# An attention and FFN kernel: the probabilities turned by way of DRAM and VectorE instead of TensorE

## The chip, the core and the metric

The kernel runs on one core of a Trainium2 chip. The time is that of one execution on the device, in microseconds (us). Lower is better. Beside the runs that are timed there is one profiled execution, from which the trace comes; its span runs from the first to the last instruction.

The core has five engines that work from queues of their own: TensorE (PE, matmuls), VectorE (DVE), ScalarE (ACT), GpSimd (POOL) and SyncE (SP), which issues all DMAs here. They wait for each other by semaphores; an instruction that waits holds up all that stand behind it on its engine.

## What is computed

One layer of a transformer on x of shape 8 x 1024 x 512, in float32: attention over segments of 128 tokens with a running memory, a residual and a layer norm, then an FFN with weights of -1, 0 and 1, a residual and a layer norm.

```python
def step(carry, inp):                      # for each of 8 segments, 8 batches, 8 heads
    mem, z = carry
    q_s, k_s, v_s = inp
    sq = jax.nn.elu(q_s) + 1.0
    att_mem = sq @ mem / (sq @ z)
    sk = jax.nn.elu(k_s) + 1.0
    mem = mem + jnp.einsum('bhlk,bhlv->bhkv', sk, v_s)
    z = z + sk.sum(axis=-2, keepdims=True).transpose(0, 1, 3, 2)
    att_dot = jax.nn.softmax(jnp.einsum('bhik,bhjk->bhij', q_s, k_s) * scale, axis=-1)
    att = att_dot @ v_s
    att = gate * att_mem + (1.0 - gate) * att
    return ((mem, z), att)
...
x = _layernorm(x + out @ Wo, axis=-1)
h = jax.nn.relu(jnp.einsum('bsd,fd->bsf', x, quantize(W1)) + b1)     # 512 -> 2048
x = _layernorm(x + jnp.einsum('bsf,df->bsd', h, quantize(W2)) + b2)
```

## The kernel before

**Tiles.** A group is one segment of two batches (`TG` = 2 tiles t of 128 tokens, 256 tokens), and there are `NG` = 32 groups. To keep the accuracy of float32, the operands of the large products are split into two float16 halves, hi and lo: one engine writes hi, another subtracts it and writes lo. The products then need two or three matmuls each.

**Stages of a group g.** `project_qk` (q and k turned, 4 banks of 24 matmuls), `project_v`, `scores`, the row maxima (`score_max`) and the exponentials into `prob`. prob stands with the queries on the partitions; the product with v in `attend` needs it with the keys on the partitions, so it is turned, split into `pt_hi` and `pt_lo`, and multiplied. `read_memory` and `update_memory` work on the running memory. The two results are gated and added (`gate_mix` on POOL) in `att_mem`; this is turned as well, split into `at`, and goes through `project_out`. After the norm (rows, y) come `ffn_up` (eight steps j, each with `h_relu` on ACT and a split by `h_split` on DVE and `h_rest` on POOL) and `ffn_down` (four pieces for each of two tiles).

**Two ways of turning.** sk, att and y are turned without TensorE: 16 DMAs on SP place the 32x32 blocks (`move_blocks`, `move_sk`), and DVE turns each block in place with one STREAM_TRANSPOSE. prob is turned on TensorE, in `turn_p` (L301 to L312): for each tile t and each half (4 heads) four transposes of 128x128 into a PSUM bank. From this bank ACT evicts `pt_hi` (L1091) and DVE writes `pt_lo` (L690).

**Order.** Each engine has one list of calls inside `for g in range(NG + 2)`; the order is written out call by call and differs from engine to engine. Calls with g - 1 and g - 2 work on earlier groups, so several groups are under way at once. In iteration g TensorE does the projections, scores, reads and `attend` of g, `project_out` of g - 1, `ffn_up` 4 to 7 and all of `ffn_down` of g - 2, and last `ffn_up` 0 to 3 of g - 1. The iteration ends with `update_memory(g)`.

**Banks.** `ffn_up` alternates between PSUM banks 0 and 1, `ffn_down` uses 6 and 7. All else takes banks 2 to 5 in turn (`take`), and waits until the previous user of the bank has been read out.

**Head.** The quantised FFN weights are made in iteration 0: 32 blocks are compared with a threshold on DVE and POOL (`compare`), turned on TensorE (`turn_w`) and evicted by ACT (`put_w`).

SP's list in an iteration is: blocks of the next x (`load_blocks`), amax to DRAM, the move of y of g - 1, amax back, the move of sk, the move of att, the two output tiles of g - 2, the load of the rows of g + 2.

## Time and profile before

| | us |
|---|---|
| median of 3 runs | 1944.64 (1944.27 to 1944.66) |
| profiled execution | 1943.67 |
| its span | 1941.8 |

The mean of TensorE's granted clock in the profiled execution was 0.982 of full speed. The trace is read as follows: a row of a timeline gives the start, the duration (of one or of several merged instructions), the engine, the line of the kernel, the operation, what it writes and reads, and how many there are. In brackets stands how long the engine had been idle and what ended that. Matmuls are pipelined: the duration of one is longer than the distance at which they follow each other. DMAs have their issue on SyncE as SPq rows; the time to landing is in a view of its own.

### The profile page before, as it was taken

Reading aid. Unit: us, or ns where it says so; the run is one execution under the profiler, and the core shown is the slowest. Engines: PE = TensorE matmul, PEld = TensorE weight load, DVE = VectorE, ACT = ScalarE, POOL = GpSimd, SP = SyncE. Lnnn points to the kernel's source line nnn. Section 1 sums busy time; section 2 is a strip of 40 time slices with the busy share of each in tenths; the row PEclk is TensorE's granted clock in tenths of the full one; section 3 lists DMA queues with packets and bytes.
Section 4 is the critical chain, followed back from the end, with each engine's and each line's share of the span. In section 5 each row is a group of like instructions: output and inputs, shape, how many; then the busy total and the mean of one; then the engine's idle time right before and its main releaser. Section 6 shows DMA issues by size and latency. Waiting matters only on the chain.

```text
span 1941.8 us, 45054 instructions
## 1 busy us (share of the span) xinstructions
PE 1868.1 (96%) x16671; PEld 1318.0 (68%) x16671; DVE 1460.8 (75%) x2991; ACT 1002.2 (52%) x2426; POOL 822.2 (42%) x806
## 2 busy tenths in 40 slices
PE   5679999999999999999999999999999999999987
PEld 3557776667777666777766677776667776667754
DVE  7877777777777777777777877777787777877753
ACT  5655455555545555555555555545554554555531
POOL 1724434434444443444454344435434444443442
PEclk9689999999999999999999999999999999999999
DMA  8422332332333233333222323323332332332221
GB/s 276 100 37 48 63 62 41 61 60 58 62 65 63 40 59 59 59 61 66 49 52 59 62 58 62 67 46 53 60 61 57 62 67 37 60 63 59 39 41 31
DMA packets 582536, 120.67 MB, mean 62 GB/s; under 512 B 555936, under 2 KB 559920, under 8 KB 581808
## 3 DMA queue, kind: packets, MB, share of 16 engines
q1 hardware_dynamic: 582320, 117.79, 30.2%
q8 instruction: 135, 2.21, 0.6%
q14 instruction: 81, 0.66, 0.2%
HBM read 50.54 MB, written 16.80 MB: 35 GB/s over the span
## 4 chain that ended last, share of the span: by engine, by line
PE 83%; SPq 6%; DVE 5%; DMA 2%; ACT 2%; issue 1%; POOL 1%; POOLq 0%; DVEq 0%; ACTq 0%
PE bank L393 11%; PE bank L394 11%; PE bank L407 9%; PE bank L408 9%; SPq L1479 6%; PE bank L263 6%; PE bank L265 6%; PE bank L264 6%; PE bank L331 3%; PE bank L374 3%; PE bank L375 3%; PE bank L376 3%; PE bank L277 2%; PE bank L310 2%; PE bank L279 2%; PE bank L278 2%
## 5 line engine op out<-in xcount | busy, mean ns | idle before, releaser
L393 PE MATMUL bank<-yt,w1t 128*128 128x256 f16 x2048 | 456.8, 274 | 5.2 <-POOL yt L1294 5.2
L394 PE MATMUL bank<-yt,w1t 128*128 128x256 f16 x2048 | 456.3, 273 | 0.0
L1126 ACT ACTIVATE arena<-bank,b_scaled,wscalars 128x256 f32<-128x256 f32 x512 | 262.9, 569 | 256.5 <-PE bank L394 232.3
L407 PE MATMUL bank<-w2t,arena 128*128 128x512 f16 x1024 | 388.4, 379 | 0.1
L408 PE MATMUL bank<-w2t,arena 128*128 128x512 f16 x1024 | 388.1, 379 | 0.0
L1080 ACT ACTIVATE prob<-bank,exp_bias,gscalars 128x128 f32<-128x128 f32 x512 | 227.1, 458 | 286.2 <-DVE exp_bias L681 277.1
L1326 POOL TENSOR_TENSOR arena<-arena 128x512 f16<-128x512 f32 x128 | 166.1, 1298 | 261.4 <-DVE arena L804 261.4
L1287 POOL TENSOR_TENSOR at<-att_dot,at 128x512 f16<-128x512 f32 x64 | 74.7, 1167 | 362.7 <-ACT at L1099 362.7
L393 PEld LDWEIGHTS bank<-yt,w1t 128*128 128x128 f16 x2048 | 201.1, 98 | 30.9 <-issue 5.6
L394 PEld LDWEIGHTS bank<-yt,w1t 128*128 128x128 f16 x2048 | 201.1, 98 | 23.1
L804 DVE CAST arena<-arena 128x512 f16<-128x512 f32 x256 | 118.5, 473 | 114.3 <-ACT arena L1126 113.1
L407 PEld LDWEIGHTS bank<-w2t,arena 128*128 128x128 f16 x1024 | 100.1, 98 | 109.1 <-issue 0.5
L408 PEld LDWEIGHTS bank<-w2t,arena 128*128 128x128 f16 x1024 | 100.2, 98 | 107.1
L807 DVE TENSOR_TENSOR arena<-arena 128x512 f16<-128x512 f32 x128 | 150.7, 1177 | 4.4
L1052 ACT ACTIVATE exp_tmp<-bank,gscalars 128x512 f32<-128x512 f32 x128 | 88.5, 692 | 115.6 <-DVE sk_t L651 114.2
L264 PE MATMUL bank<-xt,wk_hi 128*128 128x256 f16 x512 | 140.7, 275 | 0.0
L265 PE MATMUL bank<-xt,wk_lo 128*128 128x256 f16 x512 | 140.7, 275 | 0.0
L263 PE MATMUL bank<-xt,wk_hi 128*128 128x256 f16 x512 | 140.7, 275 | 0.0
L263 PE MATMUL bank<-xt,wq_hi 128*128 128x256 f16 x512 | 139.6, 273 | 0.2 <-issue 0.2
L265 PE MATMUL bank<-xt,wq_lo 128*128 128x256 f16 x512 | 139.6, 273 | 0.0
L264 PE MATMUL bank<-xt,wq_hi 128*128 128x256 f16 x512 | 139.6, 273 | 0.0
L676 DVE TENSOR_REDUCE row_max<-bank 128x4 f32<-128x512 f32 x128 | 88.0, 687 | 62.3 <-PE bank L300 62.2
(182 smaller groups left out, 4429.0 us busy)
## 6 DMA issues: line engine op xcount, KB each, us to landing
rows<-in_L_attn_x SPq DMA_DIRECT2D x32, 512.0 KB, 3.6
sk<-sk_t SPq DMA_DIRECT2D x512, 32.0 KB, 2.0
att_dot<-att_mem SPq DMA_DIRECT2D x512, 32.0 KB, 2.0
y_blocks<-rows SPq DMA_DIRECT2D x512, 32.0 KB
out_rows<-rows SPq DMA_DIRECT2D x64, 256.0 KB, 2.3
x_blocks<-in_L_attn_x SPq DMA_DIRECT2D x248, 64.0 KB, 2.8
arena<-in_L_ffn_W SPq DMA_DIRECT2D x6, 1024.0 KB, 5.8
w2t<-in_L_ffn_W SPq DMA_DIRECT2D x2, 1024.0 KB, 13.1
```

What stands on the lines that cost most here:

```text
L263: pe.matmul(ps[:, :, c], w_hi[n][:, k, cols], xt[:, :, k], start=k == 0, stop=False)
L264: pe.matmul(ps[:, :, c], w_hi[n][:, k, cols], xt[:, :, KT + k], start=False, stop=False)
L265: ins = pe.matmul(ps[:, :, c], w_lo[n][:, k, cols], xt[:, :, k], start=False, stop=k == KT - 1)
L393: pe.matmul(ps[:, c], w1t[:, k, cols], yt[:, g % 2, :, k], start=k == 0, stop=False)
L394: ins = pe.matmul(ps[:, c], w1t[:, k, cols], yt[:, g % 2, :, KT + k], start=False, stop=k == KT - 1)
L407: pe.matmul(banks[own][:], h_hi[:, f, toks], w2t[:, f, :], start=f == 0, stop=False)
L408: ins = pe.matmul(banks[own][:], h_lo[:, f, toks], w2t[:, f, :], start=False, stop=f == FT - 1)
L804: dve.tensor_copy(hi, h32[:, n % NH32]).then_inc(sem["h_hi"], 1)
L807: dve.tensor_tensor(lo, h32[:, n % NH32], hi, ALU.subtract).then_inc(sem["h_dve"], 1)
L1080: ins = act.activation(prob[:, t, at], ps[:, c], ACT.Exp, scale=gcol(g, G_EXP), bias=exp_bias[:, t, at:at + 1], accum_out=row_sum[:, t, h: ...
L1126: ins = act.activation(h32[:, n % NH32, c * GT:(c + 1) * GT], ps[:, c], ACT.Relu, scale=w(H_SCALE_Y), bias=b1_scaled[:, f:f + 1])
L1326: pool.tensor_tensor(lo, h32[:, n % NH32], hi, ALU.subtract).then_inc(sem["h_pool"], 1)
```

## The change

The probabilities no longer go through TensorE. The exponentials write `prob` in another order, `[quarter of the keys, head, 32 keys]`, so that for each query each quarter is one run of 1 KB. SP writes each tile to a tensor in DRAM, `p_dram` (`p_out`, 512 KB each), and reads both back with the blocks in their new places (`p_back`, four DMAs of 256 KB in runs of 1 KB) into `p_blocks`. DVE turns the 32x32 blocks, one STREAM_TRANSPOSE of 128x1024 for each tile. ACT then writes pt_hi in one instruction for each tile, and DVE pt_lo in four of 128x256. Both halves lie over `prob` itself, so the exponentials of the next group wait for `attend` (`pv`) instead of `turn_p`.

The lists of all five engines are new. On TensorE all eight `ffn_up` and all of `ffn_down` now belong to g - 2, `update_memory` is called for g - 1, and `attend` of both tiles follows the first piece of `ffn_down` of tile 1. The blocks 16 to 31 of the FFN weights are turned in iteration 1. `turn_y` and the split of y move to the start of the next iteration (g - 2).

```diff
-            def turn_p(g, t, half):
-                if not 0 <= g < NG:
-                    return
-                b = take(("p", g, t, half))
-                ps = banks[b][:].rearrange("p (h t) -> p h t", h=4)
-                pe.wait_ge(sem["pexp"], by_half(g, t, half))
-                for i in range(4):
-                    ins = pe.transpose(ps[:, i], prob[:, t, 4 * half + i], ident32[:])
-                ins.then_inc(sem["pturn"], 1)
-                bank_free[b] = (sem["pt"], by_half(g, t, half))
...
+            def turn_p(g, t):
+                if not 0 <= g < NG:
+                    return
+                flat_p = p_blocks[:, t].rearrange("p b f -> p (b f)")
+                dve.wait_ge(sem["pblocks"], 4 * 16 * (g + 1))
+                dve.transpose(flat_p, flat_p).then_inc(sem["pturn"], 1)
+
+            def p_split(g, t):
+                if not 0 <= g < NG:
+                    return
+                dve.wait_ge(sem["pt_hi"], by_t(g, t))
+                for b in range(4):
+                    cols = slice(32 * b, 32 * b + 32)
+                    ins = dve.scalar_tensor_tensor(out=pt_lo[:, t, :, cols], in0=p_blocks[:, t, b].rearrange("p (h n) -> p h n", h=H),
+                                                   scalar=2.0 ** 13, in1=pt_hi[:, t, :, cols], op0=ALU.mult, op1=ALU.subtract)
+                ins.then_inc(sem["pt"], 1)
...
-                    act.wait_ge(sem["pturn"], by_half(g - 1, t, half))
+                    act.wait_ge(sem["pv"], by_t(g - 1, t))
...
+            def p_out(g, t):
+
+                if not 0 <= g < NG:
+                    return
+                sp.wait_ge(sem["pexp"], by_half(g, t, 1))
+                if g:
+                    sp.wait_ge(sem["pblocks"], 4 * 16 * g)
+                sp.dma_start(p_dram[t].rearrange("b j a f -> (b j) (a f)"),
+                             prob[:, t].rearrange("p a h n -> p (a h n)")).then_inc(sem["pthere"], 16)
+
+            def p_back(g):
+                if not 0 <= g < NG:
+                    return
+                sp.wait_ge(sem["pthere"], TG * 16 * (g + 1))
+                if g:
+                    sp.wait_ge(sem["pt"], by_t(g - 1, 1))
+                for a in range(4):
+                    sp.dma_start(p_blocks[32 * a:32 * a + 32], p_dram[:, :, :, a].rearrange("t b j f -> j t b f")).then_inc(sem["pblocks"], 16)
...
+                p_out(g, 0)
+                p_out(g, 1)
```

How the lists stand in the middle of the program. First SyncE, one iteration before, from the blocks of x to the next ones (x16 is one move of blocks):

```order
L1421 DMA x_blocks<-in_L_attn_x 32x16x32 x8
L1464 DMA amax_dram<-amax 128x1
L1479 DMA y_blocks<-rows 32x8x32 x16
L1471 DMA amax_row<-amax_dram 128x128
L1491 DMA sk<-sk_t 32x8x32 x16
L1479 DMA att_dot<-att_mem 32x8x32 x16
L1512 DMA out_rows<-rows 128x512 x2
L1408 DMA rows<-in_L_attn_x 128x2x512
L1421 DMA x_blocks<-in_L_attn_x 32x16x32 x8
```

The same stretch after the change; p_dram is the tensor in DRAM, p_blocks its turned image in SBUF:

```order
L1493 DMA p_dram<-prob 128x1024 x2
L1477 DMA amax_dram<-amax 128x1
L1503 DMA p_blocks<-p_dram 32x8x256 x4
L1484 DMA amax_row<-amax_dram 128x128
L219 DMA sk<-sk_t 32x8x32 x16
L219 DMA y_blocks<-rows 32x8x32 x16
L1532 DMA out_rows<-rows 128x512
L219 DMA att_dot<-att_mem 32x8x32 x16
L1532 DMA out_rows<-rows 128x512
L1421 DMA rows<-in_L_attn_x 128x2x512
L1434 DMA x_blocks<-in_L_attn_x 32x16x32 x8
```

The write of prob and its way back stand ahead of amax_row and all three moves. The move of y has gone behind that of sk, and the first output tile stands ahead of the move of att.

Second VectorE before, from the first split of the probabilities that stands alone to the pair of the second tile; s_pt_hi is raised by ScalarE when the upper half is written, bank is PSUM:

```order
L690 SCALAR_TENSOR_TENSOR pt_lo<-bank,pt_hi 128x512 [waits s_pt_hi]
L625 STREAM_TRANSPOSE x_blocks<-x_blocks 128x512 [waits s_xblocks]
L793 STREAM_TRANSPOSE y_blocks<-y_blocks 128x512 [waits s_yblocks]
L697 RECIPROCAL inv_sum<-row_sum 128x8 [waits s_pexp]
L573 TENSOR_REDUCE gscalars<-amax_row 128x1 [waits s_back1]
L704 TENSOR_SCALAR dot_scale<-inv_sum,gscalars 128x8 [waits s_invsum,s_sc2]
L793 STREAM_TRANSPOSE y_blocks<-y_blocks 128x512 [waits s_yblocks]
L581 TENSOR_SCALAR gscalars<-gscalars 128x1 [waits s_amax_all]
L585 TENSOR_SCALAR gscalars<-gscalars 128x1 [waits s_xscale]
L690 SCALAR_TENSOR_TENSOR pt_lo<-bank,pt_hi 128x512 [waits s_pt_hi] x2
```

And after, from the split of v to the splits of the first tile (s_pblocks is raised when p_back has landed; prob is now also the name under which its two halves appear):

```order
L667 SCALAR_TENSOR_TENSOR v_lo<-bank,v_hi 128x512 [waits s_pv,s_v1] x2
L689 STREAM_TRANSPOSE p_blocks<-p_blocks 128x1024 [waits s_pblocks]
L573 TENSOR_REDUCE gscalars<-amax_row 128x1 [waits s_back1]
L812 CAST arena<-arena 128x512 [waits s_relu]
L689 STREAM_TRANSPOSE p_blocks<-p_blocks 128x1024 [waits s_pblocks]
L581 TENSOR_SCALAR gscalars<-gscalars 128x1 [waits s_amax_all]
L585 TENSOR_SCALAR gscalars<-gscalars 128x1 [waits s_xscale]
L794 TENSOR_SCALAR rows<-rows,mean_var,rstd 128x512 [waits s_rstd0]
L588 TENSOR_SCALAR gscalars<-gscalars 128x1 [waits s_xscale]
L712 TENSOR_SCALAR dot_scale<-inv_sum,gscalars 128x8 [waits s_invsum,s_sc2]
L697 SCALAR_TENSOR_TENSOR prob<-p_blocks,prob 128x8x32 [waits s_pt_hi]
L697 SCALAR_TENSOR_TENSOR prob<-p_blocks,prob 128x8x32 x3
```

The splits have moved behind two block transposes which wait for the DMAs, and the last CAST of h stands between these; the turning of y is no longer in this place.

## Rows read from the trace of the kernel before

**Rows 1.** the page, busy time and share of the span by engine, instructions

```profile
PE 1868.1 (96%) x16671; PEld 1318.0 (68%) x16671; DVE 1460.8 (75%) x2991; ACT 1002.2 (52%) x2426; POOL 822.2 (42%) x806
```

**Rows 2.** timeline of VectorE, two x maxima (start us, duration, line, what)

```profile
1039.74 1.21 DVE L560 TENSOR_REDUCE amax<-x_blocks 128x1 f32<-128x1024 f32 x1
...
1096.51 1.21 DVE L560 TENSOR_REDUCE amax<-x_blocks 128x1 f32<-128x1024 f32 x1
```

**Rows 3.** timeline of TensorE, the first matmul of iterations 2 and 32

```profile
160.09 0.28 PE L393 MATMUL bank<-yt,w1t 128*128 128x256 f16 x1
...
1867.09 0.28 PE L393 MATMUL bank<-yt,w1t 128*128 128x256 f16 x1
```

**Rows 4.** timeline of TensorE at one group of four transposes

```profile
1043.85 0.60 PE L310 MATMUL bank<-ident,prob 128*128 128x128 f32 x4
1044.29 0.38 PE L407 MATMUL bank<-w2t,arena 128*128 128x512 f16 x1
```

**Rows 5.** instructions by line and shape (total us, mean ns | idle before)

```profile
L676 DVE TENSOR_REDUCE row_max<-bank 128x4 f32<-128x512 f32 x128 | 88.0, 687 | 62.3 <-PE bank L300 62.2
...
L690 DVE SCALAR_TENSOR_TENSOR pt_lo<-bank,pt_hi 128x512 f16<-128x512 f32 x128 | 84.6, 681 | 3.2 <-ACT pt_hi L1091 3.1
...
L310 PE MATMUL bank<-ident,prob 128*128 128x128 f32 x512 | 74.3, 279 | 3.5 <-ACT prob L1080 3.5
...
L720 DVE SCALAR_TENSOR_TENSOR att_mem<-bank,gscalars,inv_den 128x256 f32<-128x256 f32 x128 | 62.0, 484 | 9.8 <-DVE inv_den L716 0.6
...
L659 DVE STREAM_TRANSPOSE sk_t<-sk_t 128x1024 f32<-128x1024 f32 x32 | 39.7, 1239 | 0.0
```

**Rows 6.** waits of TensorE: for whom, us in total, times, longest

```profile
PE bank L331 <- DVE pt_lo L690: 9.2, 8, 6.0
```

**Rows 7.** timelines of VectorE and GpSimd, the same stretch

```profile
1024.59 0.68 DVE L651 SCALAR_TENSOR_TENSOR sk_t<-exp_tmp,relu_tmp 128x512 f32<-128x512 f32 x1
...
1027.27 1.65 DVE L651 SCALAR_TENSOR_TENSOR sk_t<-exp_tmp,relu_tmp 128x512 f32<-128x512 f32 x1
...
1027.23 1.15 POOL L1287 TENSOR_TENSOR at<-att_dot,at 128x512 f16<-128x512 f32 x1 [9.96 <-ACT at L1099]
```

**Rows 8.** DMA issues: count, KB each, us from issue to landing

```profile
rows<-in_L_attn_x SPq DMA_DIRECT2D x32, 512.0 KB, 3.6
...
out_rows<-rows SPq DMA_DIRECT2D x64, 256.0 KB, 2.3
...
amax_dram<-amax SPq DMA_DIRECT2D x31, 0.5 KB, 7.3
```

**Rows 9.** timeline of SyncE's queue: moves of 16 DMAs, and x_blocks

```profile
985.12 10.39 SPq L1479 DMA_DIRECT2D y_blocks<-rows  x16
...
1053.84 11.21 SPq L1491 DMA_DIRECT2D sk<-sk_t  x16
...
1081.55 5.35 SPq L1421 DMA_DIRECT2D x_blocks<-in_L_attn_x  x8
...
1553.34 13.85 SPq L1479 DMA_DIRECT2D y_blocks<-rows  x16
```

**Rows 10.** timelines of SyncE and VectorE: the last move of att and its transposes

```profile
1863.80 11.37 SPq L1479 DMA_DIRECT2D att_dot<-att_mem  x16
...
1876.56 1.30 DVE L758 STREAM_TRANSPOSE att_dot<-att_dot 128x512 f32<-128x512 f32 x2 [3.32 <-DMA att_dot<-att_mem]
```

**Rows 11.** timeline of ScalarE: a half of the exponentials, to what follows

```profile
1039.95 0.46 ACT L1080 ACTIVATE prob<-bank,exp_bias,gscalars 128x128 f32<-128x128 f32 x1 [5.67 <-DVE exp_bias L681]
...
1041.71 0.60 ACT L1066 ACTIVATE v_hi<-bank 128x512 f16<-128x512 f32 x1
```

**Rows 12.** timeline of VectorE: the last comparisons of the weights

```profile
105.07 1.21 DVE L859 TENSOR_SCALAR yt<-arena,wscalars 128x512 f16<-128x512 f32 x2
```

**Rows 13.** timeline of TensorE: two waits near the end

```profile
1879.37 0.46 PE L374 MATMUL bank<-wo_hi,at 128*128 128x512 f16 x1 [5.12 <-POOL at L1287]
...
1905.60 0.37 PE L393 MATMUL bank<-yt,w1t 128*128 128x256 f16 x1 [5.15 <-POOL yt L1294]
```

421 lines of the change are left out of this document (209 added, 212 removed).

## The prediction

> **What bounds the kernel now.** I read the page first: its busy line, where TensorE (PE) has 96% of the span, VectorE (DVE) 75%, ScalarE (ACT) 52%, GpSimd (POOL) 42% [rows 1]. Such shares are averages, so next comes the length of one iteration of the main loop. VectorE takes the largest value of the next x once in each, and two of these in a row start 56.77 us apart [rows 2]. The first matmul of iteration 2 starts at 160.1 and that of iteration 32 at 1867.1 [rows 3]: 30 iterations in 1707.0 us, 56.90 each. So an iteration loses 0.13 us on average, and the span is a head of 160.1, 30 x 56.90, and a tail of 74.7, together 1941.8.
>
> Is TensorE streaming in these 56.77 us? The matmuls on either side of a group of four transposes follow each other with no hole: the four start at 1043.85 and the next matmul at 1044.29 [rows 4]. The view by line gives a transposition 279 ns [rows 5], but this is the latency of one; what it costs the stream is the distance, 0.44 us for four, 0.109 each. The waits of TensorE confirm it: the wait that repeats is for pt_lo, 8 times and 9.2 us, 6.0 of them in one [rows 6]. TensorE is the bound, and VectorE has about a quarter of its time free.
>
> **What the change takes off TensorE.** 16 transposes of prob per group of 256 tokens go: 16 x 0.109 = 1.74 us. With nothing else late, an iteration is 56.77 - 1.74 = 55.03 us, and 30 of them give 1707.0 - 1650.9 = 56 us. This is the top of what the steady part can give. The 279 ns of [rows 5] would promise 16 x 0.279 x 30 = 134 us, and that is not there to be had.
>
> **What it puts on VectorE.** Gone: four splits of 128x512 from PSUM, 4 x 0.681 = 2.72 us [rows 5]. New: two block transposes of 128x1024, for which the same shape on sk stands, 2 x 1.239 = 2.48 us [rows 5]; and eight splits of 128x256 whose inputs both lie in SBUF. A 128x512 of that kind took 0.68 us alone and 1.65 us when GpSimd was at work [rows 7], so eight halves cost between 8 x 0.34 = 2.7 and 8 x 0.83 = 6.6 us. I take 3.0, near the lower end, because GpSimd has nothing queued there but the gating, which waits for the attention that comes later. VectorE gets 2.5 + 3.0 - 2.7 = 2.8 us more (up to 6.4), on about 43 of 57 us: 46 to 49 of 55. It doesn't become the bound by its sum. ScalarE's four evictions become two of twice the size, about even.
>
> The trace shows GpSimd's subtraction starting at 1027.23 and the split of VectorE at 1027.27 lasting until it is over [rows 7]. The Trainium skill, "SBUF — State Buffer", Terms, says of the port pair that both share that it is "held for the full instruction" and that the loser is blocked; by that rule, with the trace agreeing, the new split is exposed to GpSimd where the old one (PSUM input) was not. If every second one met a GpSimd instruction the upper value above would hold.
>
> **The new path of the probabilities.** SyncE (SP) now issues, in each iteration, two DMAs of 512 KB to DRAM and four of 256 KB back, and its order changes; the moves of y and att_dot now stand behind them. From the last exponential to the attention: the write, two DMAs of which the second counts. A load of 512 KB lands 3.6 us after issue, a write of 256 KB to DRAM 2.3, and the 0.5 KB of amax 7.3 [rows 8]. These are the bounds; I take 3.6, the row nearest in size. The way back: four issues at the 0.67 of x_blocks (5.35 for eight [rows 9]) = 2.7, and about 3.6 to land. Then block transpose 1.24 twice, ScalarE's half about 1.2, the split 1.5: 3.6 + 2.7 + 3.6 + 2.5 + 1.2 + 1.5 = 15.1 us. Against it stands the work that TensorE has between scores(g, 1) plus some 7 us for the exponentials and attend(g, 0): from the written order one ffn_up, two project_out, memory work 1.6, three ffn_up, two project_v and five pieces of ffn_down. With 0.109 for 256 columns and twice that (0.216) for 512 this is 4 x 1.74 + 4 x 2.6 + 1.6 + 5 x 1.72 = 27.6 us. 27.6 - 7 - 15.1 leaves 5 us. This path is covered. Uncovered it would cost all 15 us in each group.
>
> **The ring that is not covered by much.** SyncE waits for the write to land before it issues anything more, and the moves are behind it. From exponentials to exponentials of the next group there is now a closed ring: write and landing 3.6; four issues 2.7; amax_row 0.6; three moves of 16 DMAs (sk, y, att); one put_out 0.5; landing of att 1.4 (the issues end at 1875.17, VectorE starts at 1876.56 [rows 10]); two transposes of att 1.3 [rows 10]; the read of the memory, two of 0.48 [rows 5] and two reciprocals, 1.3; row maximum 0.69 [rows 5] and its scaling, 1.0; 16 exponentials, four in 1.76 [rows 11], 7.0. A move takes 10.39 at its shortest, 11.21 typically, 13.85 at its longest [rows 9]; with 11.2 each the ring is 3.6 + 2.7 + 0.6 + 33.6 + 0.5 + 1.4 + 1.3 + 1.3 + 1.0 + 7.0 = 53.0 us. It is 50.6 with the shortest moves and, with 13.85 for all, 61. The slack against 55.03 is 2 us on average, and a y move of 13.85 uses it up. Before, SyncE had no such ring: att went out when its inputs were ready.
>
> I take 0.5 us per iteration for what the ring and the closer hand-overs (ffn_up now starts in the same iteration in which its y is split; project_v needs a bank that a residual frees) cost. Below stands 0. Above stand 0.6, by which the ring passes 55.03 when one of its moves takes 13.85, and 0.46, what a wait for pt_lo takes when the longest is left out, (9.2 - 6.0) / 7 [rows 6]: 1.1 together. 0.5 is near the middle, for the y move was short in half of the iterations. The iteration is 55.5 us; 30 make 1665.
>
> **Head.** 16 of the 32 weight blocks move from iteration 0 to iteration 1, and ffn_up(0) from 1 to 2. The last comparisons of VectorE ended at 106.3 [rows 12], where iteration 1 began. In the new order VectorE compares up to block 27 before the splits of iteration 1, so these start at about the same time, 105. From there iteration 1 has no FFN to fill it: to the last exponential 22 us (27 into an iteration, less the first 5), 15.1 from there to the split, 1.9 for attention and its scaling, 1.5 for xt: 105 + 40.5, say 145. y(0) is moved behind sk(1) and holds up iteration 2 by about 5. Iteration 2 starts at 150 rather than 160 (145 to 160).
>
> **Tail.** Before: 74.7 us, in which TensorE waits 5.1 for at and 5.2 for yt [rows 13]. After: iteration 32 has all eight ffn_up instead of four, 64 x 0.109 = 7.0; two memory updates 1.2; and att and y of the last groups come later relative to work that is shorter, since no projections stand before them: waits of about 16 instead of 10. 74.7 + 7.0 + 1.2 + 5.6 = 88.5.
>
> **Sum.** 150 + 1665 + 88.5 = 1903.5 us of span, against 1941.8. The profiled execution took 1943.67, 1.9 outside the span, and the median of the runs lies 1.0 above it: 1903.5 + 2.9 = 1906 us.
>
> **Rivals.** (1) *Full gain*: moves keep to 10.4 to 11.2, no wait repeats: 55.1 per iteration, 1653 + 238.5 + 2.9 = 1894, a few less with a better head. For it: the room of 5 us on the path of p. (2) *The ring is a little longer than TensorE's iteration*: 1 MB each way per group slows the moves as other traffic did for half of the y moves [rows 9]. Three moves of 12.2 make 56.0 to 56.2: 1686 + 241.4 = 1927. (3) *Slower*: the ring decides clearly. The place is SyncE's wait for p_dram. With 7.3 for the landing [rows 8] and moves of 11.5 the ring is 53.0 + 3.7 + 0.9 = 57.6 us; 30 x 57.6 + 241.4 = 1969. It decides from 56.8 per iteration on, where the sum is 1944.6. Against it: amax is 128 pieces of 4 bytes, p is rows of 4 KB, and out_rows lands in 2.3.
> The Trainium skill, "DMA: Bandwidth & Descriptors", Anatomy of one DMA, says of the completion that it "can cause a surprisingly long delay especially when the write target is HBM"; this would make (3) true. Its fit (2.0 us plus bytes over 436 GB/s) gives an estimate of 3.2 us for 512 KB, with which the ring would be 52.6; the 2.3 of out_rows agrees with the fit rather than with the warning.
> (4) *The transposes cost nothing*: excluded by [rows 4].
>
> **Chances.** Forecast (55.2 to 55.8, 1896 to 1917) 45%; full gain 17%; (2) 23%; (3) 12%; a mix that ends near the old time 3%. A measurement of this kernel can tell 0.2% from no change, some 4 us. Faster by more than that: 0.84; within 0.04; slower 0.12. The range leaves out (3), the last of (2) and the best of (1): 1884 to 1940.
>
> **What would show it.** x maxima 55.5 us apart; no L310; TensorE's idle time before ffn_up, project_v or read_memory small. If the ring decides, SyncE never waits for norm0, mixed or norm1, only for p_dram, and TensorE waits where the chain comes from att: before read_memory or scores. If p is late, VectorE waits for p_blocks and TensorE before attend. The prediction is wrong if landings of p_dram are over 6 us, if moves average above 12, or if iteration 2 starts after 165.

## The result, and the profile after

The changed kernel takes 2012.9 us (median of 4 runs, 2005.1 to 2020.0) against 1944.65 us before (median of 4 runs, 1944.3 to 1946.1): ratio 1.0345, 95% interval 1.0328 to 1.0363. It is slower by 68 us, where 1906 us was predicted, with a range of 1884 to 1940. The profiled execution has a span of 2015.1 us.

The page of the changed kernel, its busy line and its chain of work that ended last, against [rows 1]:

```profile
PE 1854.7 (92%) x16159; PEld 1260.1 (63%) x16159; DVE 1648.6 (82%) x3183; ACT 1011.6 (50%) x2362; POOL 850.3 (42%) x806
...
DVE 30%; SPq 21%; DMA 20%; PE 18%; issue 7%; ACT 2%; POOL 2%; DVEq 0%; POOLq 0%; ACTq 0%
```

The new instructions of VectorE in the view by line and shape (total us, mean ns | idle before), against [rows 5]:

```profile
L697 DVE SCALAR_TENSOR_TENSOR prob<-p_blocks,prob 128x256 f16<-128x256 f32 x256 | 90.8, 417 | 0.0
...
L689 DVE STREAM_TRANSPOSE p_blocks<-p_blocks 128x1024 f32<-128x1024 f32 x64 | 79.3, 1239 | 54.2 <-DMA p_blocks<-p_dram 54.0
```

TensorE has lost its 512 transposes and its share fell from 96% to 92%. Most of the chain no longer runs through TensorE but through VectorE, SyncE's queue (SPq) and the transfers. In the view of the waits (us in total, times, longest) one wait of TensorE repeats, and VectorE waits for the new transfer:

```profile
PE bank L411 <- POOL arena L1334: 61.7, 29, 4.5
...
DVE p_blocks L689 <- DMA p_blocks<-p_dram: 54.0, 24, 10.1
...
SPq L1484 <- DMA amax_dram<-amax: 155.4, 31, 6.9
```

L411 is ffn_down(g-2, 0, 3). It needs the half that GpSimd's h_rest(7) makes, which needs h_split(7) of VectorE, which stands in VectorE's list behind turn_p(g, 0), and turn_p waits for p_blocks. L1484 is SyncE's wait for the landing of amax_dram, ahead of the read of amax_row.

The DMA view (count, KB each, us from issue to landing) against [rows 8]:

```profile
p_dram<-prob SPq DMA_DIRECT2D x64, 512.0 KB, 2.7
p_blocks<-p_dram SPq DMA_DIRECT2D x128, 256.0 KB, 10.9
...
amax_dram<-amax SPq DMA_DIRECT2D x31, 0.5 KB, 7.9
```

The write of p, at which the prediction's third rival saw the danger, lands in 2.7 us. The way back takes 10.9, where 3.6 was taken. One iteration shows the whole path in the timelines of ScalarE (its last exponential), SyncE, VectorE, GpSimd and TensorE:

```profile
906.25 0.52 ACT L1090 ACTIVATE prob<-bank,exp_bias,gscalars 128x128 f32<-128x128 f32 x1
...
909.25 0.32 SPq L1477 DMA_DIRECT2D amax_dram<-amax  x1
909.66 2.63 SPq L1503 DMA_DIRECT2D p_blocks<-p_dram  x4
916.97 0.34 SPq L1484 DMA_DIRECT2D amax_row<-amax_dram  x1
...
924.23 1.25 DVE L689 STREAM_TRANSPOSE p_blocks<-p_blocks 128x1024 f32<-128x1024 f32 x1 [2.10 <-DMA p_blocks<-p_dram]
...
929.39 1.41 DVE L697 SCALAR_TENSOR_TENSOR prob<-p_blocks,prob 128x256 f16<-128x256 f32 x4
...
926.05 1.16 POOL L1334 TENSOR_TENSOR arena<-arena 128x512 f16<-128x512 f32 x1 [5.67 <-DVE arena L812]
...
927.36 0.38 PE L411 MATMUL bank<-w2t,arena 128*128 128x512 f16 x1 [2.74 <-POOL arena L1334]
```

From the end of the last exponential (906.8) to the end of the last split (930.8) it takes 24.0 us, not 15.1: 2.9 until p_back is issued, 14.6 until the last block has landed and 6.6 for turns and splits, against 3.6, 6.3 and 5.2 of the prediction. The x maxima of the iteration before this one start at 846.13 and 908.01, 61.9 us apart. In it TensorE waited 4.5 us at L411. The stretches of that iteration behind the wait (length, busy times with counts, mean granted clock, DMA share, GB/s) show the second part of the price:

```profile
864.00:868.00 4.00, 0.75 (x3) 0.37 (x4) 3.84 (x10) 2.00 (x2) 1.16 (x1) 0.95 0.43 59
868.00:872.00 4.00, 4.00 (x13) 1.46 (x12) 2.69 (x9) 1.45 (x3) 0.00 (x0) 0.62 0.30 49
872.00:876.00 4.00, 4.00 (x62) 2.58 (x61) 2.61 (x3) 0.00 (x0) 1.70 (x1) 1.00 0.28 47
```

TensorE stood idle for most of 864 to 868; from 868 to 872 the granted clock is 0.62, that is 1.2 GHz for the larger part of it, then 2.4 GHz again. The sixteen matmuls of the piece behind the wait took 5.30 us, against 3.61 in the iteration shown above, where the wait had been 2.7 us. So this stall cost 4.5 + 1.7 us.

The iterations are not alike. From the fourth x maximum (193.77) to the last (1843.37) lie 28 of them, 58.91 each. From the fifth on they come in fours, with means of 60.2, 58.0, 60.6, 57.5, 59.2 and 57.1 us. p_blocks follows with the same period. The view of the tile p_blocks over one long iteration (window 908 to 920) and over one short (1082 to 1094):

```profile
DMA to landing us min/median/max: 10.9/11.3/12.4
...
DMA to landing us min/median/max: 7.7/8.7/10.2
```

Eight is the number of 512-byte rows of amax_dram in 4 KB. In the long iterations the row g + 1 that is written has g + 1 = 4 to 7 modulo 8. Runs e5 and e6 follow from this observation.

The same trace holds a second hint. The last group has no next x, so no write of amax_dram stands ahead of its reads. The view of p_blocks there (window 1903 to 1907):

```profile
DMA to landing us min/median/max: 3.8/4.9/5.7
```

It proves nothing by itself, for near the end other transfers are missing too, but it points at the small write.

### The profile page after: what moved, and what is told of

Read it like the earlier page. It is cut to its first block, busy times and chain, and to the rows that moved or that the text cites. A ratio compares the mean times of both kernels' runs of the same rounds, so it can differ in the third digit from the quotient of the medians.

```text
span 2015.1 us, 44191 instructions
## 1 busy us (share of the span) xinstructions
PE 1854.7 (92%) x16159; PEld 1260.1 (63%) x16159; DVE 1648.6 (82%) x3183; ACT 1011.6 (50%) x2362; POOL 850.3 (42%) x806
## 4 chain that ended last, share of the span: by engine, by line
DVE 30%; SPq 21%; DMA 20%; PE 18%; issue 7%; ACT 2%; POOL 2%; DVEq 0%; POOLq 0%; ACTq 0%
SPq L219 18%; DMA p_blocks<-p_dram 14%; PE bank L411 4%; PE bank L412 4%; DVE row_max L676 3%; DVE xt L631 3%; DVE stats L785 3%; DMA att_dot<-att_mem 2%; DMA amax_dram<-amax 2%; DVE exp_bias L681 2%; DVE arena L812 2%; SPq L1503 2%; PE bank L397 2%; DVE rows L781 2%; PE bank L398 2%
## 5 line engine op out<-in xcount | busy, mean ns | idle before, releaser
L411 PE MATMUL bank<-w2t,arena 128*128 128x512 f16 x1024 | 399.1, 390 | 61.7 <-POOL arena L1334 61.7
L412 PE MATMUL bank<-w2t,arena 128*128 128x512 f16 x1024 | 399.1, 390 | 0.0
L1334 POOL TENSOR_TENSOR arena<-arena 128x512 f16<-128x512 f32 x128 | 160.4, 1253 | 236.2 <-DVE arena L812 235.0
L411 PEld LDWEIGHTS bank<-w2t,arena 128*128 128x128 f16 x1024 | 102.3, 100 | 192.7 <-issue 87.8
L1057 ACT ACTIVATE k_hi<-bank 128x512 f16<-128x512 f32 x64 | 38.2, 597 | 330.4 <-PE bank L280 330.4
L1269 POOL TENSOR_TENSOR att_dot<-att_dot,gate_out 128x512 f32<-128x512 f32 x64 | 94.6, 1478 | 212.6 <-DVE att_dot L740 212.6
L812 DVE CAST arena<-arena 128x512 f16<-128x512 f32 x256 | 169.2, 671 | 12.5 <-ACT arena L1134 12.5
L412 PEld LDWEIGHTS bank<-w2t,arena 128*128 128x128 f16 x1024 | 102.3, 100 | 117.5 <-issue 12.5
L815 DVE TENSOR_TENSOR arena<-arena 128x512 f16<-128x512 f32 x128 | 170.9, 1335 | 4.4
L278 PE MATMUL bank<-xt,wk_hi 128*128 128x256 f16 x512 | 144.1, 281 | 6.3 <-DVE xt L631 3.4
L279 PE MATMUL bank<-xt,wk_hi 128*128 128x256 f16 x512 | 144.1, 281 | 0.0
L1098 ACT ACTIVATE prob<-p_blocks 128x1024 f16<-128x1024 f32 x64 | 67.5, 1056 | 145.1 <-DVE p_blocks L689 145.1
## 6 DMA issues: line engine op xcount, KB each, us to landing
p_blocks<-p_dram SPq DMA_DIRECT2D x128, 256.0 KB, 10.9
```

Source lines behind the costliest of these rows:

```text
L278: pe.matmul(ps[:, :, c], w_hi[n][:, k, cols], xt[:, :, k], start=k == 0, stop=False)
L279: pe.matmul(ps[:, :, c], w_hi[n][:, k, cols], xt[:, :, KT + k], start=False, stop=False)
L411: pe.matmul(banks[own][:], h_hi[:, f, toks], w2t[:, f, :], start=f == 0, stop=False)
L412: ins = pe.matmul(banks[own][:], h_lo[:, f, toks], w2t[:, f, :], start=False, stop=f == FT - 1)
L812: dve.tensor_copy(hi, h32[:, n % NH32]).then_inc(sem["h_hi"], 1)
L815: dve.tensor_tensor(lo, h32[:, n % NH32], hi, ALU.subtract).then_inc(sem["h_dve"], 1)
```

## The experiments

Names: the *ring* is SyncE's closed chain of the prediction; *p's path* is exponentials, p_dram, p_blocks, turn_p, split, attend. Two questions are asked in turn: which of the two holds up TensorE, and what makes the transfers late. The table gives the runs in order. "Base" is the kernel that each edit is made on; all are compared with the kernel before on the same chip. The period is the mean distance of the x maxima from the fourth on.

| run | base | edit | us | ratio to before, 95% | period |
|---|---|---|---|---|---|
| e1 | changed | amax_row asked for in the middle of sk | 2059.4 | 1.0594 (1.0567 to 1.0621) | 60.60 |
| e2 | changed | h_split(7) ahead of turn_p(0) | 1993.0 | 1.0243 (1.0221 to 1.0265) | 57.98 |
| e3 | changed | y's move from ScalarE's queue | 2022.1 | 1.0408 (1.0382 to 1.0433) | 58.94 |
| e4 | e2 | and amax_row as in e1 | 2020.9 | 1.0382 (1.0354 to 1.0410) | 59.21 |
| e5 | e2 | amax_dram's rows all at offset 0 of 4 KB | 1976.4 | 1.0152 (1.0133 to 1.0172) | 57.55 |
| e6 | e2 | all at offset 2048 | 2022.7 | 1.0384 (1.0369 to 1.0400) | 59.00 |
| e7 | e2 | amax_dram behind p_back, all_max later | 2096.7 | 1.0760 (1.0728 to 1.0793) | 61.67 |
| e8 | e2 | p_back by t | 1979.5 | 1.0163 (1.0148 to 1.0178) | 57.77 |
| e9 | e7 | amax_row behind sk | 1933.9 | 0.9938 (0.9921 to 0.9954) | 56.17 |
| e10 | e9 | y's move from ScalarE's queue | 2017.5 | 1.0373 (1.0357 to 1.0388) | 58.93 |
| e11 | e9 | h_split(7) back behind turn_p(0) | 1935.1 | 0.9932 (0.9916 to 0.9949) | 56.19 |
| e12 | changed | SyncE's order of e9 alone | 2105.3 | 1.0806 (1.0789 to 1.0822) | 62.07 |
| e13 | e2 | amax_dram in 2 elements of 256 bytes, a constant | 1913.4 | 0.9833 (0.9817 to 0.9849) | 55.71 |
| e14 | e9 | amax_dram ahead of p_back again | 2040.9 | 1.0492 (1.0472 to 1.0513) | 59.74 |
| e15 | e2 | amax_dram in 4 elements of 128 bytes | 1919.7 | 0.9869 (0.9855 to 0.9884) | 55.85 |
| e16 | changed | the same | 1938.1 | 0.9964 (0.9950 to 0.9979) | 56.55 |
| e17 | before | the same | 1934.2 | 0.9905 (0.9889 to 0.9922) | 56.77 |

### Is it the ring, or p's path? (e1 to e4)

The first theory was that the ring had grown by amax_row's wait for amax_dram's landing, 5.0 us in each iteration, which the prediction's sum of the ring doesn't hold.

```diff
-                move_blocks(sp, in_k(sk[:]), sk_t, sem["skblocks"])
+                move_blocks(sp, in_k(sk[:]), sk_t, sem["skblocks"], range(2))
+                if g:
+                    bounce_back(g + 1)
+                move_blocks(sp, in_k(sk[:]), sk_t, sem["skblocks"], range(2, 4))
```

> Edit: amax_row is asked for in the middle of sk's sixteen transfers, after eight of them, instead of ahead of all of them; nothing else. Theory R (the ring on SyncE decides, and amax_row's wait for the landing of amax_dram, 155.4 us in 31 waits, 5.0 in each iteration, stands in it): the wait is covered by eight transfers of sk (8 x 0.65 = 5.2 us), the ring falls from 58.9 to 53.9 us, TensorE decides again with 55.5 us or so per iteration, and the time is 2013 - 28 x 3.4 = 1918 us (1905 to 1940). Theory P (what decides is the landing of p_blocks, 10.9 us, which holds turn_p and behind it the half h_split(7) on VectorE, for which ffn_down waits 61.7 us in all): p's transfers stand ahead of amax_row and keep their times, so the time stays within 10 us of 2013 us. Theory C (VectorE and GpSimd disturb each other, VectorE 188 us busier than before): no change, 2013 us.

46 us slower than the changed kernel instead of 95 faster. The wait is gone from SyncE's list, but the timeline of SyncE in e1 shows that the time it was waiting had not been free:

```profile
928.59 2.79 SPq L1503 DMA_DIRECT2D p_blocks<-p_dram  x4
931.49 11.76 SPq L219 DMA_DIRECT2D sk<-sk_t  x8
943.34 0.73 SPq L1484 DMA_DIRECT2D amax_row<-amax_dram  x1
```

Sixteen transfers of a quiet move are issued in 10.4 us, 0.65 each. Here the first eight took 11.8 us: they now stand right behind p_blocks' reads and the small write. (In e15 below, sk stands as close behind the same reads, and its sixteen are issued in 10.4.) amax_row was issued 14.8 us after p_back's first issue instead of 7.3, VectorE waited for it in all_max (38.3 us in all), and h_split(7) stands behind all_max: TensorE's wait at L411 grew from 61.7 to 108.9 us.

```diff
                 v_split(g, 1)
+                h_split(g - 2, 7)
                 turn_p(g, 0)
                 all_max(g + 1)
-                h_split(g - 2, 7)
```

> Edit: on VectorE h_split(g-2, 7) stands ahead of turn_p(g, 0) instead of behind it; nothing else. Theory P (the wait of turn_p for p_blocks holds h_split(7), and through GpSimd's h_rest(7) TensorE's ffn_down(g-2, 0, 3)): the 61.7 us of that wait vanish, 2013 - 62 = 1951 us (1945 to 1965). Theory R (the ring on SyncE decides): TensorE's waits at this place vanish but come back at the next point where it meets the ring (scores, attend or k's projection), and the time stays at 2013 us (2003 to 2020).

20 us faster: L411 no longer waits, but the stall comes back in part at attend, which follows it in TensorE's list. The waits of TensorE in e2:

```profile
PE bank L349 <- issue: 40.4, 41, 3.9
```

L349 is attend. "issue" means that the view names nobody; in the kernel attend waits for `pt`, the split of the same p_blocks. So p's path is late by itself, and h_split(7) was only the first to show it. In e4, with both edits, that is the one wait left in the middle of the iteration (79.7 us, 57 times).

```diff
-                sp.wait_ge(sem["norm0"], by_t(g, 1))
+                act.wait_ge(sem["norm0"], by_t(g, 1))
...
-                move_blocks(sp, in_k(y_blocks[:]), in_k(rows[:, g % NX]), sem["yblocks"])
+                move_blocks(act, in_k(y_blocks[:]), in_k(rows[:, g % NX]), sem["yblocks"])
...
                 xt_hi(g + 1, 0)
                 xt_hi(g + 1, 1)
+                move_y(g - 1)
```

> Edit: y's sixteen transfers are issued from ScalarE's queue, behind xt_hi of the next group, where ScalarE stood idle for 9.4 us, instead of from SyncE's between sk and att; nothing else. Theory R: 11.4 us leave the ring (58.9 to 47.5 us), TensorE decides with about 55.5 us, perhaps 1 more since ScalarE issues for 10.4 us where it had 9.4 and k's halves come later: 2013 - 28 x 3 = 1929 us (1905 to 1945). Theory P or C: y's move isn't on p's path and VectorE's work is the same, so 2013 us within 10, or slower by ScalarE's 10.4 us.

9 us slower, with 11 us per iteration taken out of the ring, and TensorE's wait at L411 is as long as before (60.3 us against 61.7). So the ring is not what bounds the changed kernel. ScalarE's 10.4 us of issues fill what was free (9.4 to 11.1 us), and the halves of k come a little later (VectorE's wait for them grows from 8.1 to 23.9 us).

> Both edits: amax_row in the middle of sk's transfers, and h_split(g-2, 7) ahead of turn_p(g, 0). Theory R: as with the first edit alone, 1918 us, and up to 15 less where the p_blocks wait still held ffn_down once the ring is short: 1903 to 1920. Theory P: 1951 us, as with the second edit alone. If each edit alone does nothing and both together do, two rings of about the same length decide together.

2020.9 us, neither theory's number: 28 us above e2, so amax_row's new place costs here too. In e4 a long iteration shows the price of a wait at attend in the timeline of TensorE and in the stretches around it (length, busy times with counts, granted clock, DMA share, GB/s):

```profile
866.56 0.19 PE L349 MATMUL bank<-v_hi,prob 128*128 128x64 f16 x1 [3.26 <-issue]
```

```profile
866.00:868.00 2.00, 0.90 (x26) 0.83 (x27) 2.00 (x8) 1.34 (x2) 0.00 (x0) 0.99 0.30 49
868.00:870.00 2.00, 2.00 (x26) 1.49 (x27) 2.00 (x3) 0.00 (x0) 1.46 (x1) 0.50 0.30 49
870.00:872.00 2.00, 2.00 (x7) 0.77 (x6) 2.00 (x6) 0.00 (x0) 1.78 (x2) 0.65 0.35 57
```

From 868 to 870 the granted clock is 0.50, 1.2 GHz. The two attends took 0.86 and 1.43 us (0.85 each undisturbed) and the 24 matmuls of ffn_down behind them 6.41 instead of 5.35: 1.6 us on top of the 3.8 of waits.

### What makes p_blocks late? (e5 to e8)

```diff
-        amax_dram = nc.dram_tensor("amax_dram", [NG, P], F32, kind="Internal").ap()
+        amax_dram = nc.dram_tensor("amax_dram", [NG, 8, P], F32, kind="Internal").ap()[:, 0]
```

and in e6

```diff
+        amax_dram = nc.dram_tensor("amax_dram", [NG, 8, P], F32, kind="Internal").ap()[:, 4]
```

> On the kernel with h_split(7) first (1993 us): amax_dram's rows stand 4096 bytes apart instead of 512, all at the offset of row 0; no instruction is moved. What it tells apart: in the changed kernel p_blocks takes 11 to 12.6 us to land where amax_dram's row g+1 has g+1 = 4 to 7 modulo 8, and 7.7 to 9.4 us where it has 0 to 3; the iterations follow with 60 and 57 us. Theory A (the 512 bytes of amax_dram, written in elements of 4 bytes just ahead of p's reads, get in their way, by their place in 4 KB of DRAM): all iterations become like the short ones, 14 x 2.2 us less, 1962 us (1950 to 1972), and p_blocks lands in 8 to 9.5 us everywhere. Theory O (the pattern of eight comes from something else): 1993 us within 6, the pattern stays.

> As the run before it, but all rows of amax_dram at the offset of row 4 (2048 bytes) in their 4096. Theory A: all iterations become like the long ones, 14 x 2.2 us more, 2024 us (2012 to 2035), p_blocks lands in 11 to 12.6 us everywhere. Theory O: 1993 us within 6, and the pattern of eight stays.

Not one instruction differs between the two, only addresses of 512 bytes per group, and 46 us lie between them. (Offsets are counted from the start of the tensor.) The pattern of eight is gone in both. e6 came out as expected, e5 is 4 us above its range. Landing of p_blocks from 1000 to 1500 us, e5:

```profile
DMA to landing us min/median/max: 5.9/8.3/10.7
```

and e6:

```profile
DMA to landing us min/median/max: 10.1/11.6/13.4
```

So the small write of amax_dram disturbs the 1 MB of reads that is issued right behind it. In e5 TensorE hardly waits at attend any more (6.9 us, 8 times, against 40.4 in e2), yet the time is only 17 us below e2: something else is nearly as long. e7 puts the write behind the reads:

```diff
                 turn_p(g, 0)
-                all_max(g + 1)
...
                 p_split(g, 1)
+                all_max(g + 1)
+                for level in range(4):
+                    x_scale(g + 1, level)
                 att_scale(g, 0)
...
                 p_out(g, 1)
+                p_back(g)
                 bounce_out(g + 1)
...
-                p_back(g)
                 bounce_back(g + 1)
```

> On the kernel with h_split(7) first (1993 us): amax_dram is written behind p_back's four issues instead of ahead of them, and on VectorE all_max and the four steps of x_scale stand behind p_split(g, 1), since amax_row then comes 3 us later. Theory A: p_blocks' reads are out ahead of the write in elements of 4 bytes, land in 7 to 9 us in all iterations, attend's stalls and the lower clock behind them go, and TensorE keeps 56.0 to 56.5 us per iteration: 1993 - 28 x 1.6 = 1948 us (1940 to 1965). Theory O, or a landing that the reads in runs of 1 KB take by themselves: 1993 us within 8, or up to 28 us slower if the later xt holds k's projection by 1 us.

The landing fell to 4.3 us, below the 7 to 9 that were expected. The time rose by 104 us all the same. Waits of TensorE, VectorE and SyncE in e7:

```profile
PE bank L397 <- POOL yt L1300: 137.0, 32, 7.4
...
DVE y_blocks L801 <- DMA y_blocks<-rows: 135.7, 30, 5.9
...
SPq L1482 <- DMA amax_dram<-amax: 267.5, 31, 9.7
```

Here the ring does decide. SyncE waits 8.6 us for the write in each iteration, nothing hides it, and sk, y and att stand behind: a period of 61.7 us, with TensorE waiting for y's split.

> On the kernel with h_split(7) first (1993 us): p_back by t, four reads of 128 KB for t = 0 ahead of amax_dram's write and as soon as its write has landed, four for t = 1 behind it, with a semaphore for each; the bytes are the same, four issues (2.6 us of SyncE) more. Theory P (the length of p's path from the last exponential to attend decides): the half for t = 0 is issued some 2 us earlier and lands some 4 us earlier, so attend(g, 0) no longer waits, and only t = 1 can: 1993 - 28 x 1.2 = 1960 us (1945 to 1975). Theory R (SyncE's ring decides): 2.6 us more in each iteration, 1993 + 73 = 2066 us.

13 us faster than e2, where theory P gave 33. Attend no longer waits (5.0 us, 3 times, against 40.4), but most of that gain is lost again at y: VectorE's wait for the move of y is 35.7 us (25 times) and TensorE's for its split 29.6, against 14.1 in e2.

The prediction's own sign tells how close the ring is. When SyncE still waits for norm1 ahead of an output tile, the ring has slack. That wait and the one for amax_dram, from 300 to 1700 us, first in the changed kernel:

```profile
SPq L1484 <- DMA amax_dram<-amax: 121.2, 24, 6.9
SPq L1532 <- DVE rows L794: 21.3, 20, 2.6
```

and in e8:

```profile
SPq L1484 <- DMA amax_dram<-amax: 111.3, 24, 5.7
SPq L1532 <- DVE rows L794: 1.1, 4, 0.3
```

In e2 the second row is 4.0 us (9 times), in e5 0.8 (2 times), in e7 it is missing. So the changed kernel's ring is about 1 us shorter than its iteration, and once p's path is relieved (e2, e5, e8) the ring decides with 57.5 to 58.0 us. The prediction's ring of 53.0 with SyncE's wait for amax_dram added fits the periods: 53.0 + 5.0 = 58.0 against 57.98 in e2, and 53.0 + 8.6 = 61.6 against 61.67 in e7.

### Both at once (e9 to e12)

```diff
-                bounce_back(g + 1)
                 if g == 0:
+                    bounce_back(g + 1)
                     gates_out()
...
                 move_sk(g)
+                if g:
+                    bounce_back(g + 1)
                 move_y(g - 1)
```

> On the run with amax_dram behind p_back (2097 us, p_blocks lands in 4.3 us, SyncE waits 8.6 us in each iteration for amax_dram's landing): amax_row is asked for behind sk's sixteen transfers, which cover that wait. Theory A+R (p's path is held by amax_dram's write while it stands ahead of p's reads, and the ring on SyncE, with its wait for that write, stands right behind it): SyncE's ring falls from 62 to 53 us, p's landing stays at 4 to 5 us, and TensorE decides with its own 55.1 to 56.2 us: 2097 - 28 x 6 = 1929 us (1905 to 1945), below the kernel before. Theory D (VectorE, disturbed by GpSimd, with 50 of 57 us busy and a fixed order, is next): 57 us per iteration, 1960 us. Theory R alone would give the same as A+R here; it fell with the first run.

1933.9 us, 163 us below e7 by the place of one transfer. The page of e9:

```profile
PE 1834.8 (95%) x16159; PEld 1252.1 (65%) x16159; DVE 1667.7 (86%) x3183; ACT 1005.8 (52%) x2362; POOL 834.6 (43%) x806
```

VectorE is busier here than in the changed kernel (1648.6), so its load and its contention with GpSimd are not what made that one slow.

> The same, and y's sixteen transfers from ScalarE's queue behind xt_hi. Theory A+R: SyncE's ring falls to 42 us and no longer matters; the time is that of the run before it or up to 10 us less where sk, y and att were still late, 1920 to 1945 us. Theory D: 1960 us in both, the ring being no limit in either.

84 us slower than e9. In e9 ScalarE stood idle for only 7.0 us behind xt_hi, not for the 9.4 of the changed kernel, and sixteen transfers take some 10.4 to issue. So the halves of k come late: VectorE's wait for them (k_lo) grows from 7.3 to 78.4 us and TensorE's for yt from 15.3 to 82.8.

> The fast version (1934 us) with h_split(7) back at its place of the changed kernel, behind turn_p(g, 0). Theory A+R (h_split(7) was late only because turn_p waited for p_blocks' landing): with a landing of 4.6 us turn_p no longer waits, so the place costs at most turn_p's own 1.24 us, of which TensorE sees nothing: 1934 us (1930 to 1940). Theory P2 (VectorE's order around h_split(7) costs by itself): 20 us as between the changed kernel and the one with h_split(7) first, 1954 us.

1935.1 us: in this order the place of h_split(7) costs nothing that can be measured.

> The changed kernel with SyncE's order alone mended: p_back ahead of amax_dram, amax_row behind sk; VectorE's order is the changed kernel's, with all_max between turn_p(g, 0) and h_split(7). amax_row then lands some 17 us behind p_back's first issue, where all_max stood 13 us behind it. Theory A+R: p_blocks lands in 4.5 us as before, but all_max now holds VectorE for 4 us in each iteration ahead of h_split(7) and p_split, so ffn_down and attend wait: 2000 to 2040 us; both queues must be mended together. Theory S (the landing on SyncE's side is all that matters): 1934 to 1945 us.

2105.3 us, above even the upper end I gave. p_blocks is early, but all_max stands in VectorE's list between turn_p(0) and h_split(7) and waits 116.7 us in 31 times for amax_row; TensorE's wait at L411 is 129.3 us. SyncE's and VectorE's lists have to be changed together.

### Is it the elements of 4 bytes? (e13 to e17)

```diff
-                sp.dma_start(amax_dram[g], amax[:, g % 2]).then_inc(s_there[g % 2], 16)
+                sp.dma_start(amax_dram[g].rearrange("(r c) -> r c", r=2), sixteen[0:2, :]).then_inc(s_there[g % 2], 16)
```

> On the kernel with h_split(7) first (1993 us): amax_dram's write, still ahead of p's reads, has two elements of 256 bytes in place of 128 of 4 bytes. Its source is a constant 16.0, so the scale of x is not that of the reference; all other work is the same. Theory E (it is the 128 elements of 4 bytes that hold the reads behind them): the write lands in some 2.5 us instead of 8, p_blocks in 4 to 5 us instead of 10.9, SyncE's wait for the write is covered by p_back's issues, so both paths are short at once, and the time is 1925 to 1945 us. Theory W (any write to this place ahead of the reads does it): 1993 us within 15, p_blocks lands in 9 us or more.

> The fast version (1934 us) with one thing undone: amax_dram's write stands ahead of p_back's four issues again (some 3 us earlier); amax_row behind sk and VectorE's order stay. Theory A+R: p_blocks lands in 9 to 12 us again, in the pattern of eight, sk's transfers are issued more slowly behind it, attend waits in the long iterations: 1934 + 28 x 1.6 = 1979 us (1955 to 2000). Theory D2 (the gain of the fast version came from amax_row's place and VectorE's order alone): 1934 us within 5.

The landing of p_blocks in e13 and in e14, from their DMA views:

```profile
p_blocks<-p_dram SPq DMA_DIRECT2D x128, 256.0 KB, 4.7
...
p_blocks<-p_dram SPq DMA_DIRECT2D x128, 256.0 KB, 10.9
```

e13 has e2's order, amax_dram ahead of p's reads, and is 80 us faster than e2, below its range of 1925 to 1945. e14 moves one instruction of 0.3 us in e9 and is 107 us slower. I had expected 45: not only p_blocks was late, 7.5 to 12.5 us again in the pattern of eight, but sk's sixteen issues took up to 18.4 us, so amax_row and xt were late too. So it is not any write at this place that does the harm, but this write with its 128 elements of 4 bytes. e13 leaves out the true scale of x; here is the whole computation with that one write in four elements:

```diff
+                    dve.wait_ge(sem["amax_part"], g)
+                    dve.transpose(amax[:, g % 2], amax[:, g % 2]).then_inc(sem["amax"], 1)
...
-                sp.dma_start(amax_dram[g], amax[:, g % 2]).then_inc(s_there[g % 2], 16)
+                sp.dma_start(amax_dram[g].rearrange("(r c) -> r c", r=4), amax[0:P:32, g % 2]).then_inc(s_there[g % 2], 16)
```

> The whole computation again: VectorE turns the column of maxima in blocks of 32 (one block transpose of 128x32), and amax_dram is written as four elements of 128 bytes from partitions 0, 32, 64, 96, at its old place ahead of p's reads; on the kernel with h_split(7) first (1993 us). Theory E: as with two elements of 256 bytes, 1913 us, plus 28 x 0.3 us of VectorE that TensorE doesn't see: 1910 to 1922 us. Theory that below 512 bytes each element costs as one of 4 bytes does, and their number tells nothing: 1993 us.

> The changed kernel with this one thing, the write of amax_dram in four elements of 128 bytes, and h_split(7) at its old place behind turn_p. Theory E (the 128 elements of 4 bytes explain the whole of the loss): 1912 to 1925 us, the 20 us of h_split(7)'s place having been its wait for the same landing. Theory E+P2 (its place costs by itself): 1935 us.

e15 is 1919.7 us, inside its range of 1910 to 1922 and 1.3% faster than the kernel before. Its page, busy line and chain:

```profile
PE 1829.9 (95%) x16159; PEld 1259.4 (66%) x16159; DVE 1659.7 (87%) x3214; ACT 1007.9 (53%) x2362; POOL 848.0 (44%) x807
...
PE 50%; DVE 31%; SPq 8%; issue 6%; DMA 2%; ACT 1%; DVEq 1%; POOL 0%; POOLq 0%; ACTq 0%
```

two x maxima in the timeline of VectorE:

```profile
1412.24 1.21 DVE L560 TENSOR_REDUCE amax<-x_blocks 128x1 f32<-128x1024 f32 x1
...
1468.10 1.20 DVE L560 TENSOR_REDUCE amax<-x_blocks 128x1 f32<-128x1024 f32 x1
```

and the landing of p_blocks from 1000 to 1500 us:

```profile
DMA to landing us min/median/max: 3.3/4.7/6.1
```

TensorE is the largest part of the chain again. SyncE doesn't wait for amax_dram in e15 at all, so the one edit shortens p's path and the ring together. e16 is the changed kernel with this write alone: 75 us faster than the changed kernel, which had lost 68. The 18 us between e16 and e15 are h_split(7)'s own place: in e16 turn_p(0), all_max's chain and its neighbours run ahead of it even when nothing waits (L411 still waits 17.0 us, 29 times). In e11 all_max doesn't stand there; L411 waits 11.9 us, and yet the time is e9's. Why the place costs in one order and not in the other is not shown.

> The kernel before, with the same write of amax_dram in four elements of 128 bytes (and VectorE's block transpose of 128x32). It tells how much of the distance between the mended change (1919.7 us) and the kernel before is the change's own. Theory E: in the kernel before nothing large is queued behind that write, and SyncE waited for it once in 31 times, since the eleven microseconds of y's move stood between; the time stays, 1945 us within 4, and the mended change is 1.3% faster by its own. Rival: the elements of 4 bytes also delayed y's and sk's transfers there, 1930 to 1940 us.

The kernel before gains too, by 1% (18 us on this chip), where theory E expected nothing; the rival's 1930 to 1940 us came true. Its x maxima are 56.8 us apart everywhere, and the first three intervals are 38.8, 80.8 and 56.4 instead of 39.4, 83.4 and 59.4. Between the spans of the two traces lie 9 of the 18 us (the kernel before was traced in another set of runs); the rest is not shown.

Each set of runs has its own runs of the kernel before (1943.8 us for e15 and e16, 1952.3 for e17), so ratios are what can best be compared: 0.9869 for e15, 0.9905 for e17, 0.9964 for e16. With the write mended in both, the change costs 0.6% as it stands (e16) and gives 0.4% with h_split(7) moved (e15), each within some 0.2%. By the times alone it gives 0.7% (1919.7 against 1934.2), and the period falls from 56.77 to 55.85 us.

## Why the prediction was wrong

The prediction's sum can be laid beside the traces stage by stage. In the changed kernel iteration 2 starts at 161.9 (first matmul of project_qk), iteration 32 at 1928.0 (first of update_memory), and the span ends at 2015.1.

| | predicted | changed kernel | e15 |
|---|---|---|---|
| head | 150 | 161.9 | 153.2 |
| 30 iterations | 55.5 each | 58.87 each | 55.88 each |
| tail | 88.5 | 87.1 | 87.9 |
| span | 1903.5 | 2015.1 | 1917.5 |

- **TensorE decides, and its transposes are worth 0.109 us each** [rows 4]. Right in the main. An iteration of e15 is 55.8 us with 0.3 us of waits in it, so 55.5 without, against 55.03 in the sum and 56.77 with the transposes [rows 2]. So 1.2 of the 1.74 us came off TensorE; what takes the other 0.5 is not shown.
- **VectorE's load.** The new instructions came out as summed: the transposes 1.24 each, the eight halves 8 x 0.417 = 3.3 us, against 3.0. VectorE gained 188 us in all, where 2.8 x 32 = 90 was predicted. The rest lies in old instructions. Five groups of the view by line, against the same ones of before, gained 50.7 us (the CASTs of h), 30.1 (exp_bias), 21.1 (one step of the scalars), 20.2 (the subtraction behind the CASTs) and 19.7 (xt); others lost a little. That they now run beside GpSimd is likely, but no run separates it. e9 and e15 carry this load and are fast.
- **The path of p: this step failed.** "And about 3.6 to land. [...] This path is covered", with 5 us of room. The row it stood on was that of rows<-in, a transfer with no such write ahead of it. p_blocks took 10.9 us, 7.3 more, against a room of 5. It was that term of the sum and not the way of reckoning: with the landing at 4.8 us the path is covered, as the prediction says. In the iteration shown the whole path was 8.9 us longer than summed, 3.9 more than its room; the average iteration lost 3.4 (58.9 against 55.5). The loss is made of waits at L411 (61.7 us in all), not at attend as the path alone would have it, since h_split(7) stands behind turn_p, and of the lower clock behind the longer ones.
- **The ring: a term was missing.** Its sum of 53.0 takes amax_row as 0.6 us of issue and leaves out SyncE's wait for amax_dram's landing, 5.0 us in each iteration (155.4 in 31). With it the ring is 58.0, 3 us above TensorE's 55.03, so the forecast would have failed even with p's path covered: e2, e5 and e8 have periods of 57.98, 57.55 and 57.77. Rival 3 (1969 us) saw a ring that decides, but put it at SyncE's wait for p_dram, which is 3.6 us in 4 times, hidden by the wait for the next x maximum. In the changed kernel itself p's path was the longer of the two.
- **amax_dram.** Both failures are this one write, and the row that held the answer was on the table: 7.3 us for 0.5 KB [rows 8]. I used it twice, as an upper bound for p_dram's landing and then to dismiss that bound ("amax is 128 pieces of 4 bytes, p is rows of 4 KB"). I didn't ask what it does to a transfer queued behind it. In the kernel before, y's move of 11.2 us stood between the write and amax_row and hid the wait; the change moves y away.
- **The fit of rival 3.** The Trainium skill, "DMA: Bandwidth & Descriptors", Anatomy of one DMA, gives it for DMAs that are issued from GpSimd, while these are issued by SyncE. The estimate of 3.2 us for 512 KB stands against 2.7 measured.
- **Head.** 12 us too short. 8.7 of them are gone in e15, where the first p_blocks lands in 7.7 us instead of 15.5; 3.2 remain.
- **Tail.** Right within 1.4 us, with the waits of 6.8 and 7.4 for yt that the "16 instead of 10" meant.
- **What would show it.** "If p is late, VectorE waits for p_blocks and TensorE before attend" was the sign that came true; TensorE waited one place earlier, at ffn_down(0, 3), and at attend once that was out of the way. None of the three numbers that were to refute the prediction came true: p_dram landed in 2.7 us and not over 6, the moves averaged 11.2 to 11.3 and not above 12, iteration 2 started at 161.9 and not after 165. The landing of p_blocks was not among them.

Left open: why the 4-byte elements hold up reads of other addresses behind them, and why their place in 4 KB matters. The Trainium skill, "DMA: Bandwidth & Descriptors", Specifications, says that below 512 bytes the DMA engine "does read-modify-write", and, in Rules for kernel authors, that a last dimension that isn't contiguous becomes one descriptor for each element. The 128 descriptors agree with e13 and e15, where fewer elements did no harm. The Trainium skill doesn't say there what such a write does to transfers behind it. Elements of 256 and 128 bytes (e13, e15) are below 512 too and do no harm, so being below 512 bytes is not enough. From e2 to e15 the size of the elements, their number and the number of partitions that they come from change together; no run here tells which of the three matters, or where between 4 and 128 bytes, or between 128 and 4 elements, it turns.

## What to carry to other kernels

In this kernel a transfer of a few hundred bytes that landed late (7.3 us) was the warning. Take such a row as a warning for whatever is queued behind it, not only for whoever waits for it: look for the small transfer with the long landing before you put a large one behind, and write a column as few long elements, after a block transpose of VectorE that costs 0.2 us. When a wait is hidden by something that the change moves away, it belongs in the new sum. Name the landing of every new transfer among the numbers that would refute you, the way back as well as the way out. And when two chains are of nearly equal length, mending one shows the other: here moving the write cured p's path and cost 104 us (e7), and the second edit, which without it makes the kernel slower (e14, 2041 us against e2's 1993), brought 163 back (e9).

## What the runs showed of the hardware

- 128 elements of 4 bytes written to DRAM took 7.3 to 9.6 us to land, and made 1 MB of reads issued just behind them land in 10.9 us. With the write behind the reads, or ahead of them in 2 or 4 elements, they landed in 4.3 to 4.9.
- The same write, with its rows 4096 bytes apart, cost less at offset 0 (8.3 us median landing of the reads, e5) than at offset 2048 (11.6 us, e6).
- SyncE's issues themselves slow down behind such traffic: eight in 11.8 us against 0.65 us each (e1), sixteen in up to 18.4 us (e14) against 10.4 (e15).
- After 2.7 us of idle TensorE the next sixteen matmuls took 3.61 us and the granted clock stayed at 1.00; after 4.5 us idle they took 5.30, with 0.62 over 4 us; after 3.3 us idle (e4) the clock was 0.50 for 2 us. Over the whole span the mean granted clock was 0.965 in the changed kernel, 0.982 before.
- Issuing from ScalarE's queue costs ScalarE about the same 0.65 us for each transfer: sixteen of them where it had 7.0 us free cost the kernel 84 us (e10).
